# Eight batches through attention, FFN, local attention and FFN: a loop of merged passes against one order written out over all batches

## The reference

```python
x = x + attn_a(_layernorm(x), Wq, Wk, Wv, Wo)        # 16 heads of 8, rope, causal over 256 rows
x = x + ffn(_layernorm(x), w_gate, w_up, w_down)     # 128 -> 352 -> 128, silu(gate) * up
x = x + attn_b(_layernorm(x), w_qkv, ln_w, w_proj)   # 16 heads of 8, causal inside groups of 32 rows
x = x + ffn(_layernorm(x), w_gate, w_up, w_down)     # the same weights again

def fp4_linear(x, w):      # both sides are rounded to FP4 in blocks of 16 first
    xq, wq = fp4_quant_dequant(x), fp4_quant_dequant(w)
    return jnp.einsum('bsk,nk->bsn', xq, wq)
```

## Time and profile before

| | us |
|---|---|
| median of 3 runs | 627.68 |
| lowest and highest run | 624.8, 632.15 |
| the profiled execution: its span, from the first to the last instruction | 621.5 |
| DVE busy in it | 354.9 |
| PE busy in it | 387.6 |
| ACT busy, POOL busy | 203.7, 168.9 |

### The profile page before, as it was taken

How to read it: one execution, slowest core, us unless ns; L and a number is a source line. 1 busy time by engine, 2 the same in 40 slices (tenths; PEclk the granted TensorE clock), 3 DMA queues, 4 the chain that set the end, 5 groups by cost and what they waited for, 6 DMA issues and landing times.

```text
span 621.5 us, 11084 instructions
## 1 busy us (share of the span) xinstructions
PE 387.6 (62%) x4031; PEld 249.4 (40%) x4061; DVE 354.9 (57%) x950; ACT 203.7 (33%) x548; POOL 168.9 (27%) x210
## 2 busy tenths in 40 slices
PE   0316656756966796678677866785788438516533
PEld 0214434534543554455444544454445324303312
DVE  3406667267249844985497449755954637431532
ACT  1000603512640374146404640564155204302300
POOL 6110210430243044214430443143222212320201
PEclk9957969968895999599968996998689759955955
DMA  5050140072018002800370037004600130040000
GB/s 170 0 120 2 32 90 2 23 159 47 1 52 170 6 2 65 165 3 0 88 141 3 0 84 146 3 0 102 122 4 2 45 66 3 9 102 2 10 0 8
DMA packets 61951, 31.84 MB, mean 51 GB/s; under 512 B 3360, under 2 KB 61664, under 8 KB 61920
## 3 DMA queue, kind: packets, MB, share of 16 engines
q1 hardware_dynamic: 61920, 31.42, 22.9%
HBM read 17.19 MB, written 13.63 MB: 50 GB/s over the span
## 4 chain that ended last, share of the span: by engine, by line
PE 44%; DVE 25%; issue 8%; DMA 6%; POOL 6%; ACT 6%; SPq 4%; POOLq 0%; DVEq 0%; ACTq 0%
PE bank L619 6%; PE bank L637 4%; PE bank L517 3%; PE bank L585 3%; PE bank L577 3%; PE bank L502 3%; PE bank L465 3%; DMA Kl<-scr_l 2%; DVE bmax L972 2%; PE bank L432 2%; PE bank L444 2%; PE bank L506 2%; PE bank L630 2%; PE bank L572 2%; PE bank L541 2%
## 5 line engine op out<-in xcount | busy, mean ns | idle before, releaser
L972 DVE TENSOR_REDUCE bmax<-bank 128x3 f32<-128x384 f32 x128 | 63.0, 552 | 24.1 <-PE bank L487 22.8
L693 ACT ACTIVATE prob<-bank 128x384 f32<-128x384 f32 x128 | 55.9, 490 | 12.1 <-PE bank L506 11.0
L483 PE MATMUL bank<-Kf,Qf 128*128 128x128 bf16 x128 | 23.5, 281 | 53.9 <-DMA Kf<-scr_f 45.7
L828 POOL TENSOR_TENSOR fa__w<-fa__w,fa__c 128x256 f32<-128x256 f32 (+1 forms) x16 | 19.2, 1202 | 116.4 <-DVE fa__w L932 116.4
L828 POOL TENSOR_TENSOR fb__w<-fb__w,fb__c 128x256 f32<-128x256 f32 (+1 forms) x16 | 19.9, 1242 | 92.9 <-DVE fb__w L932 92.9
L733 ACT ACTIVATE probl<-bank 128x512 f32<-128x512 f32 x64 | 38.3, 599 | 19.2 <-PE bank L577 18.1
L483 PEld LDWEIGHTS bank<-Kf,Qf 128*128 128x128 bf16 x128 | 10.1, 113 | 72.5 <-DMA Kf<-scr_f 30.9
L485 PE MATMUL bank<-Kf,Qf 128*128 128x256 bf16 x128 | 35.5, 374 | 0.0
L487 PE MATMUL bank<-maskb,identb 128*128 128x256 bf16 x128 | 34.9, 369 | 0.0
L577 PE MATMUL bank<-Ql,Kl 51*128 51x128 bf16 x256 | 26.1, 224 | 11.7 <-DMA Ql<-nmTl 9.5
L656 ACT ACTIVATE fa__xqT<-bank 128x256 f32<-128x256 f32 x8 | 3.1, 385 | 84.1 <-PE bank L432 84.1
(11 more groups left out here) (208 smaller groups left out, 966.4 us busy)
## 6 DMA issues: line engine op xcount, KB each, us to landing
scr_f<-partsf SPq DMA_DIRECT2D x16, 192.0 KB, 2.3
Qf<-scr_f SPq DMA_DIRECT2D x16, 192.0 KB
Kf<-scr_f SPq DMA_DIRECT2D x16, 192.0 KB
scr_l<-partsl SPq DMA_DIRECT2D x16, 192.0 KB, 3.4
Ql<-scr_l SPq DMA_DIRECT2D x16, 192.0 KB, 3.6
Kl<-scr_l SPq DMA_DIRECT2D x16, 192.0 KB, 4.9
scr_f<-partsf SPq DMA_DIRECT2D x16, 128.0 KB, 2.0
scr_l<-partsl SPq DMA_DIRECT2D x16, 128.0 KB, 2.2
```

The source lines that it names most:

```text
L693: act.activation(prob[:, h % 8, :], bank[h % 3][:, 0:384], ACT.Exp).then_inc(f.s_exp, 1)
L828: pool.tensor_tensor(w.w[:, 0:n], w.w[:, 0:n], w.c[:, 0:n], ALU.subtract).then_inc(dif, 1)
L972: dve.tensor_reduce(bmax[:, h, :], bank[h % 4][:, 0:384].rearrange("p (n k) -> p n k", k=P), AX.X, ALU.max).then_inc(bmax_done, 1)
```

## The change

The loop and the passes go. All stages of all batches are generators with bare yields, and for each engine one table gives every piece of every batch its place in one order over the whole kernel (a line per batch). A batch's stages are no longer bound to a pass. The x of all batches is loaded ahead into one tile `xall`, in which each block adds its result in place, and from which the output is stored. The stacks Qf, Kf, Ql, Kl and the tile Vl have two homes, used by even and odd batches. The two FFNs take the banks 6 and 7 in turns given by a list: each turn waits for the half before it in that list. The local attention moves to the banks 4 and 5. The rounding of an FFN's input gets tiles of its own (xu, xc, xw, xscale). The rows that load the masks and the first weights use fa, fu and fg, so maskf and wraw go. The FFN weights' rounding is in the DVE table as pieces 0 to 16.

```diff
-F1K = dict(load=-47.98, ln=-112.26, turn=-33.14, qkv=-5.62, rope=9.99, split=65.11, fetch=31.52)
...
+FFN_TURNS = [
+    ("a", 0, "up"), ("a", 0, "down"), ("a", 1, "up"), ("a", 1, "down"),
+    ("a", 2, "up"), ("a", 2, "down"), ("a", 3, "up"), ("a", 3, "down"),
+    ("b", 0, "up"), ("b", 0, "down"), ("a", 4, "up"), ("a", 4, "down"),
...
+    ("b", 3, "up"), ("b", 3, "down"), ("a", 7, "up"), ("a", 7, "down"),
+    ("b", 4, "up"), ("b", 4, "down"), ("b", 5, "up"), ("b", 5, "down"),
+    ("b", 6, "up"), ("b", 6, "down"), ("b", 7, "up"), ("b", 7, "down"),
+]
+TIMES = {
...
+    "pe.local2": """
...
+347 351 362 363 365 366 368 370 371 373 374 375 376 377
+378 380 390 391 393 396 398 400 402 403 405 406 407 408
+409 411 415 416 418 420 421 423 424 425 426 427 428 429""",
...
+    "dve.weights": """
+0 2 3 4 5 6 7 8 10 11 13 15 16""",
...
+    "dve.front2": """
+18 19 20 21 22 23 24 25 26 27 28 29 30 31 32 33 34 38 39
+41 42 43 44 45 46 47 48 49 50 51 52 53 54 55 56 58 68 70
+72 73 74 75 76 77 78 79 80 81 82 83 84 85 86 87 89 105 107
+109 110 111 112 113 114 115 116 117 118 119 120 121 122 123 124 126 142 145
+147 148 149 150 156 157 158 159 160 161 164 165 166 169 170 172 174 194 196
+199 200 201 202 203 204 211 212 214 215 216 217 221 222 223 225 227 245 247
+251 252 253 255 261 263 265 266 267 268 270 271 272 273 274 275 277 295 299
+302 303 304 305 310 313 314 315 316 317 320 322 323 325 326 328 330 348 350""",
...
-def merge(*threads):
-
-    done = 1e9
-    at = [next(t, done) for t in threads]
-    while min(at) < done:
-        n = at.index(min(at))
-        at[n] = next(threads[n], done)
+def weave(engine, threads):
+
+    steps = []
+    for n, (stage, b, thread) in enumerate(threads):
+        next(thread)
+        at = TIMES[engine + "." + stage].splitlines()[1 + b].split()
+        steps += [(float(t), n, k) for k, t in enumerate(at)]
+    for _, n, _ in sorted(steps):
+        next(threads[n][2], None)
...
-        xin = sb("xin", [P, T, D])
-        xres = sb("xres", [P, T, D])
+        xall = sb("xall", [P, NBATCH, T, D])
...
-        Qf = sb("Qf", [P, H, SEQ], BF16)
-        Kf = sb("Kf", [P, PAIRS, SEQ], BF16)
+        Qfs = [sb(f"Qf{i}", [P, H, SEQ], BF16) for i in range(2)]
+        Kfs = [sb(f"Kf{i}", [P, PAIRS, SEQ], BF16) for i in range(2)]
...
+        def turn_before(w, b, phase):
+
+            n = FFN_TURNS.index(("a" if w is ffn_a else "b", b, phase))
+            if n == 0:
+                return None
+            name, b0, phase0 = FFN_TURNS[n - 1]
+            w0 = ffn_a if name == "a" else ffn_b
+            return (w0.s_h_ready if phase0 == "up" else w0.s_done), T * (b0 + 1)
...
-            for s in range(LAG):
-                one(s)
-            with eng.Fori(LAG, NBATCH) as s:
-                one(s)
-            for s in range(NBATCH, NBATCH + LAG):
-                one(s)
+        def passes(engine, **stages):
+
+            threads = []
+            for stage, thread in stages.items():
+                threads += [(stage, b, thread(b)) for b in range(1 if stage == "weights" else NBATCH)]
+            weave(engine, threads)
...
+            sp.dma_start(res(1), batch(x, 1)).then_inc(x_loaded[1], 16)
             sp.wait_ge(fw_zero, 1)
...
+            for b in range(2, NBATCH):
+                sp.dma_start(res(b), batch(x, b)).then_inc(x_loaded[b], 16)
...
-                if later(b):
-                    sp.wait_ge(f.s_st_ps, b * H)
+                if b > 1:
+                    sp.wait_ge(f.s_st_ps, (b - 1) * H)
...
             def local1(b):
-                yield L1K["turn"]
+                yield
                 pe.wait_ge(l.s_xn, b + 1)
-                if later(b):
+                if b > 0:
+                    pe.wait_ge(l.s_nmT, b)
+                    if b > 1:
+                        pe.wait_ge(l.s_done, b - 1)
...
                         if u == 0:
                             pe.wait_ge(l.s_nm_loaded, (b + 1) * 32)
+                            if b < NBATCH - 1:
+                                pe.wait_ge(l.s_rest, b + 2)
...
-                elif both:
-                    pe.wait_ge(ffn_a.s_h_ready, T * (b + 3))
-                turn(bank[5], w.xq).then_inc(w.s_xqT_ps, 1)
+                if (turn_of := turn_before(w, b, "up")) is not None:
+                    pe.wait_ge(*turn_of)
+                turn(bank[6], w.xq).then_inc(w.s_xqT_ps, 1)
...
-            pool.memset(Kf[:, :, :], 1.0)
-            pool.memset(Qf[:, :, :], 0.0)
+            for tile in Kfs:
+                pool.memset(tile[:, :, :], 1.0)
+            for tile in Qfs:
+                pool.memset(tile[:, :, :], 0.0)
...
-                pool.wait_ge(l.s_xn, b + 1)
-                pool.tensor_tensor(flat(xlres), flat(xl), zeros[:, :], ALU.add).then_inc(xl_placed, 1)
...
-                link(ins)
-                dve.tensor_copy(rs[:, 0, :], stats[:, :, 0])
...
-                link(dve.tensor_copy(xl[:, :, :], x2[:, :, :]))
-                moments(link, l, xl, stl, mvl, rsl)
+                moments(link, l, res(b), stl, mvl)
...
-                link(dve.tensor_copy(w.x[:, :, :], w.src[:, :, :]))
-                moments(link, w, w.x, w.st, w.mv, w.rs)
+                moments(link, w, res(b), w.st, w.mv)
```

More of the change, by code:

```diff
@@ new lines @@
+TIMES = {
+    "sp.front1": """
+0 1
+3 4
+6 7
+9 10
+14 16
+20 22
+28 30
+35 37""",
+    "sp.front2": """
+2
+5
+8
+13
+19
+27
+34
+43""",
+    "sp.local1": """
+11 12
+17 18
+23 24
+29 31
+36 38
+41 42
+45 47
+49 50""",
+    "sp.local2": """
+15
+21
+26
+32
+39
+44
+48
+52""",
+    "sp.store": """
+25
+33
+40
+46
+51
+53
+54
+55""",
+    "pe.weights": """
+2""",
+    "pe.front1": """
+0 1
+11 12
+35 36
+65 66
+100 101
+151 152
+210 211
+265 266""",
+    "pe.front2": """
[7 rows of a table added]
+301 302 305 306 313 315 317 321 328 332 333 335 339 341 343 346 349 350 352 354 356 357""",
+    "pe.local1": """
@@ new lines @@
+285 287 291 304 307 308 312
+342 344 348 359 360 361 364
+384 385 386 392 394 395 397
+399 401 404 410 412 413 414
+417 419 422 430 431 432 433
+434 435 436 437 438 439 440""",
+    "act.weights": """
+4""",
+    "act.front1": """
+0 1 2 3
+5 6 8 11
+31 32 34 37
+62 63 65 68
+97 98 100 103
+149 150 152 173
+206 207 209 212
+260 261 263 266""",
+    "act.front2": """
[7 rows of a table added]
+325 329 330 331 333 334 335 337 338 339 340 342 343 345 347 348 349 351 352 353 355 358""",
+    "act.local1": """
+80 87 92 94
+118 123 128 130
@@ new lines @@
+398 400 404 407 409
+412 415 419 426 427
+428 429 430 431 432""",
+    "pool.front1": """
+0 2 3 4
+5 6 7 8
+9 12 13 15
+16 20 21 24
+25 31 32 33
+35 44 47 50
+51 59 60 63
+65 73 74 75""",
+    "pool.front2": """
+1
+10
+17
+27
+38
+52
+68
+81""",
+    "pool.local1": """
+23 26 29
+36 37 41
+43 49 53
+54 58 66
+67 72 78
+80 85 86
+90 92 95
+101 102 104""",
+    "pool.ffn_a1": """
+11 14
+19 22
+30 34
+40 42
+56 57
+70 71
+83 84
+94 96""",
+    "pool.ffn_a2": """
+18
+28
+39
+45
+62
+77
+88
+98""",
+    "pool.ffn_b1": """
@@ new lines @@
+46 48
+61 64
+76 79
+87 89
+91 97
+99 100
+106 107
+109 110""",
+    "pool.ffn_b2": """
+55
+69
+82
+93
+103
+105
+108
+111""",
+    "dve.weights": """
+0 2 3 4 5 6 7 8 10 11 13 15 16""",
+    "dve.front1": """
+1 9 12
+14 17 35
+36 37 59
+60 63 90
+91 98 127
+132 135 175
+186 189 228
+238 241 278""",
+    "dve.front2": """
[7 rows of a table added]
+302 303 304 305 310 313 314 315 316 317 320 322 323 325 326 328 330 348 350""",
+    "dve.local1": """
+96 97 103 106
+134 136 141 144
+162 179 187 190
+191 218 232 234
+240 264 280 284
@@ new lines @@
+290 291 318 321
+339 340 353 355
+376 378 382 384""",
+    "dve.local2": """
+129 168 176
+180 208 213
+219 250 254
+257 297 301
+306 334 341
+344 365 367
+370 390 392
+395 406 407""",
+    "dve.ffn_a1": """
+40 57 61 62
+71 88 92 94
+108 125 128 130
+146 151 153 155
+198 205 207 209
+249 256 258 260
+300 307 309 311
+352 356 358 360""",
+    "dve.ffn_a2": """
+64 65 66 67 69 93 95
+99 100 101 102 104 131 133
+137 138 139 140 143 152 154
+163 167 171 173 177 182 184
+220 224 226 229 231 236 239
@@ L399, in ffn2 @@
[L399 to L406 removed]
+                yield
+                if b > 1:
+                    sp.wait_ge(l.s_st_ps, (b - 1) * 2 * GROUPS)
+                fetch(b, l, scr_l, Qls[b % 2], Kls[b % 2])
```

660 lines of the change are left out of this document (355 added, 305 removed), and 28 rows, old and new, of tables (FFN_TURNS, TIMES).

## The result

| | before | after |
|---|---|---|
| median of the runs | 626.24 us (623.13 to 632.15, 4 runs) | 606.73 us (604.98 to 609.7, 4 runs) |
| profiled span | 621.5 us | 603.9 us |
| granted TensorE clock over the span | 0.834 | 0.815 |

The ratio is 0.9692, with a 95% interval of 0.9622 to 0.9763: 3% faster, where the prediction said 521 us and a range of 487 to 565. The direction is right, four fifths of the gain did not come. A run of after takes 1.8 us more than its own profiled span (605.69 against 603.9).

A forecast was written before the change was run, and what follows sets the result against it. Neither TensorE nor VectorE alone was the bound; each step laid their phases end to end. Start 78.7, light steps 116, full steps 196 and end 124 sum to 514.7, plus 6: 521 us, range 487 to 565.

The forecast's parts named there:

- The loop: Hardware loop's edge: crossed under cover of VectorE's maxima, so removing it saves 0 to 2 us in all, taken as 0.
- The two homes: Stacks with two homes: TensorE's 3.94 us wait per step before the first score, and the slow clock behind it, go.
- covered with 3.6 us to spare: Setup: POOL's four more memsets end by 19.9 us, before TensorE's need at 23.5; first residual add stays at 78.7 us.
- 1.5 us a step: Full steps: VectorE and POOL pieces meeting more often cost 0 to 3 us per step, 1.5 counted inside the 49.
- 13 us less by the copies: VectorE: dropped copies save 1.7 us of its work per batch, 13 us in all.
- The light steps: First three steps after batch 0's first residual add: front's latency decides, 38, 38 and 40 us, 116 in all.
- I take 49, nearest to the two FFN turns: Four full steps: 49 us each, VectorE 85% busy, bounds 43 and 58; 196 us in all.
- 22 to 24 us: Length of one FFN turn on banks 6 and 7; two make 44 to 48 us in every step.
- rival A: FFN turns stay at 28 to 30 us without overlap, full step 57, total 561 us; chance 0.22.
- 6.0 of fa's 29.9 us: Argument against the slow-turn rival: 6.0 us of the loop's FFN turn were waiting while the other FFN held the banks.
- four turns of 22: End, behind the last first residual add: FFN chain of 8 plus four turns of 22 is 96, then b7; end 124 us.
- The 6 us on top: Added to the summed span because the runs' median, 627.7 us, was 6.2 above the profiled span.

The follow-up runs named there:

- e1: The kernel before, with the hardware loop over steps 4 to 7 written out as four steps: 626.69 us against 626.89, ratio 1.0.
- e2: The kernel after, with fills of the second Qf, Kf, Kl and Vl moved behind POOL's first root of batch 1: 602.14 us, ratio 0.9591.
- e5: The kernel after with only the TIMES tables changed, another merged order from a list scheduler, same turn list: 555.55 us, ratio 0.8892.
- e8: The kernel after with second-home fills moved later, FFN turns overlapped from batch 3 on, and a longer-searched merged order: 524.83 us, ratio 0.8371.
- e4: The kernel after, with four more VectorE multiplies of 128x512 behind the rope multiplies of batches 1 to 7: 622.4 us, ratio 0.9909.
- e10: The kernel after, with POOL's last multiply of each FFN turn done three times, +2.77 us a turn: 630.3 us, ratio 1.0056.
- e7: The kernel after in its own order, with 111 extra unused TensorE matmuls at 29 places inside FFN turns: 591.34 us, ratio 0.945.

## Why the prediction was wrong, and where it was right

**The loop: right.** Nothing, as the earlier trace rows said and e1 measured. By the Trainium skill (Runtime: NRT & Kernel Launch, Instruction fetch mechanics), a taken branch to code that has not been fetched stalls the engine, so the edges should have shown; here they do not, within 2.4 us.

**The two homes: right.** TensorE's wait for Kf fell from 45.7 to 10.4 us, 7.65 of it for the first batch, and the first scores' matmuls from 0.28 to 0.24 us.

**The start: wrong step "covered with 3.6 us to spare".** I compared POOL's last fill with TensorE's first need and did not ask what VectorE does in those 9 us. It does three short conversions, which took 0.2 to 1.1 us in before and e2, and last until POOL's fills let them through in after. Measured: 12 us late instead of 0, of which e2 gives back 5.5. The order of e5 gives back 9.5 with all fills in place (x1(0) ends at 81.1): the order decides how much of a late start is felt. The Trainium skill (SBUF — State Buffer, Who interferes with whom) says that whichever of GpSimd and VectorE issues first keeps the shared port pair for its whole instruction and the other stands. The trace agrees in kind: the cast at 11.98 ends 0.55 us behind the fill that it met. It goes further in length: the piece that began at 15.97 ended at 19.87, behind the second of two Kl fills that follow each other without a pause. I had weighed this for the steady part only, at 1.5 us a step. There too it was too small: VectorE should have been busy for 13 us less by the copies and was busy for 9 more, although its instructions are nearly the same otherwise, so some 22 us of lengthening over the span, 2.8 a batch; a group that shows it, after and before (line engine op, count, busy us, mean ns):

```profile
L1201 DVE TENSOR_SCALAR fb__xn<-xall,fb__mv,fb__rs 128x128 f32<-128x128 f32 x16 | 12.4, 815 | 2.7 <-POOL fb__rs L1062 2.7
```

```profile
L916 DVE TENSOR_SCALAR fb__xn<-fb__x,fb__mv,fb__rs 128x128 f32<-128x128 f32 x16 | 4.8, 341 | 1.1 <-POOL fb__rs L785 1.1
```

What these 22 us cost in time was not tried apart. In e5 VectorE's total is 359.1, so the order also decides how often the two engines meet.

**The light steps: the right kind, 9 us short.** 39.5, 41.1 and 44.6 us against 38, 38 and 40. e5 and e8 needed 111.6 and 119.7 for the three (81.1 to 192.7 and 74.3 to 194.0), on either side of my 116.

**The full steps: the step "I take 49, nearest to the two FFN turns" failed**, by the 22 to 24 us that it put into a turn. The mechanism was rival A's, told there with its price: turns of 28 to 30 us without overlap, 57 a step. Measured are 29.1 a turn and 58.8 a step, just above my upper bound of 58. The rows behind the 22 to 24 give 24.1, a turn that finds all engines free, and 23.9; the 22 has no row. A turn that meets other stages' work is longer even in the better order: e5, with its turns one behind the other as the change has them, needs 26.4 a turn and 53.8 a step. The smallest parts of after add up to 19.7, but no turn had them together; the shortest took 24.8. In a queue written out in advance every hand-over of the relay (VectorE, POOL, TensorE, ScalarE) can come in behind another stage's piece. I argued against A that 6.0 of fa's 29.9 us were waiting for the other FFN and would go. They went, and waiting behind other stages came in their place. I also priced the three chains as amounts of work; e4 and e10 show that in this fixed order two chains that are each only partly full both pass on over half of a delay, 15.7 of 22.8 us and 23.6 of 41.5.

**The end: the step "four turns of 22" failed.** It is 153 us against 124. Behind x1(7) the rest of turn b3 took 13.3 us and not 8, the next four turns 112.7 (28.2 each) and not 88, and b7 24.8 where I had 26. The clock is a second thing that I never asked about. The lone FFN of rows 8 itself ran at a granted clock of 0.50 (595.0 to 619.2 of before), so a low clock is not what makes the 28.2 longer than its 24.1; but it could be had back: e7 took 17 us off the end, where its last five turns take 24.3 us each in place of 27.5.

**The 6 us on top: mis-sized, at no great cost.** A run takes 1.8 us more than its own span; the other 4 of the 6 came from comparing the median with the span of a shorter run. So the pieces are 89 us short and the predicted time 86.

**How near the floor is.** With the change's own list of turns, one behind the other, the best order tried takes 547 to 561 us (e5). e8, the same tiles and the same work with fills moved, overlapped turns and another order, takes 524.8 us with full steps of 49.3 where 49 stood. That this is close to 521 does not confirm the sum, since the 49 was made of serial turns. What was wrong was to take the order that was given as one that comes near what the resources allow, and to price turns that no longer lie in each other's quantisation, 32 phases in a row, by the time of one that runs alone.

**What stays open.** Why the given order is as poor as it is: shown is that the order alone costs 51 to 58 us, and where a turn loses (the table), but not which rows of the tables are to blame. How much of that is itself the clock (0.815 in after, 0.873 in e5) was not separated; for scale, e7 raised it to 0.886 in the given order and gained 15 us.

## What to carry to other kernels

When stages are laid over each other in fixed queues, look for the resource that they take in turn, multiply its number of turns by the length of a turn as measured in company and not alone, and check that product against the sum before anything else. A long written-out order is a part of the kernel like any other and worth an experiment of its own: with every instruction kept, another order was worth 51 us or more here, where the change with the order that it came with brought 19.5. And a setup is not hidden because its last consumer comes late; ask what the neighbouring engine does in the meantime.

## What the runs showed of the hardware

- Beside POOL's fills two short VectorE instructions of 0.2 us took 3.8 to 3.9 us (after), and two normalisations of 0.3 us each took 7.96 us together (e2), through fills that followed one another without a pause. VectorE's score maxima, read from PSUM, were not stretched beside POOL's other work: of the 128 in after 41 ran beside a POOL instruction, and none took over 0.56 us. No run has them beside a fill.
- 111 matmuls of no use made the kernel 15 us faster, most of it at the end, where the granted clock went from 0.64 to 0.83: the four gate/up matmuls fell from 2.67 to 1.45 us, the six down matmuls from 1.65 to 0.94.
